# Vision tower with a mixture-of-experts layer on one core: last tiles reordered on ScalarE and GpSimd, weight casts moved behind the search, bias rows moved behind the gates, zero fill moved from step 18 to step 6

## The chip, the cores and the metric

The kernel runs on 1 core of one Trainium2 chip. The metric is the device time of one launch in microseconds. Three runs of the kernel before took 414.73, 414.69 and 413.27 us, a median of 414.69 us.

## What is computed

64 images are cut into 36 patches each, normalized, projected to 256 features, normalized again, and given a class row and position rows. That makes 37 rows per image, 2368 in all. Then come one attention layer and one layer of eight experts:

```python
h = tok(x)                                        # 64 x 37 rows of 256
xa = layernorm(h)
attn = where(eye, -max, (q / 256) @ k.T)          # per image, its own row is masked
h = h + softmax(attn) @ v
x2 = layernorm(h)
probs = softmax(x2 @ router_w + router_b); topv, topi = top_k(probs, 2)
# each expert takes at most 444 (row, slot) pairs, those with the highest gates
hid = gelu(xin @ w1 + b1); out_e = (hid @ w2 + b2) * gate
out = layernorm(scatter_add(out_e)) * ln_g + ln_b
return h + out
```

## The kernel before, in words

**Tiles and steps.** Three images make a tile of 111 rows, so there are 22 tiles (`TILES`). A software pipeline of 28 steps (`SKEW` is 6) works on up to seven tiles at once; every engine has its own `step(i, slot)`, written out by hand, and `pipeline` unrolls the first and last steps and loops over the middle ones. The engines meet at semaphores only, and each engine does its instructions in the written order. In step i, tile i is projected and tile i - 1 is normalized for attention (L636). Tile i - 2 has its scores and its exponential (L666), tile i - 3 its attention output (L1246), and tile i - 4 its second normalization: logits L654, row L595. Its residual row then gets the last bias `ln_b` on GpSimd (L1624, called bias row here).

**SyncE's queue.** One queue in one order carries the loads of x and nearly all stores of the first part. Step i loads tile i + 4 (L442, three pieces of 36 rows) into the buffer that tile i has left (four buffers). It then stores the second normalization of tile i - 4 (L487) and the residual rows of tile i - 6 twice (L506 into `x2_rows`, L509 into `out`). One step also has the zero fill: the two zero blocks (L496), one row of `sums` (L498), and rows 112 to 127 of all 46 blocks of `x2_rows` (L499, from 16 partitions of `zero`). VectorE takes the statistics of tile i + 3 in step i (L1080), in the middle of its step:

```python
                t = i + 3
                if live(t):
                    stats_x(t, (slot + 3) % 4)
```

**Routing.** From step 21 on VectorE also picks each row's two best experts (`best`, L1132 to L1145) and makes the gates (`gates`, L1150 to L1162). This is done for the first 16 tiles within the steps and for the last six behind them. A search in eight rounds then finds each expert's threshold. In a round VectorE counts one part of the keys (L1290) and ScalarE the other (`signs_of`, L707 and L710). The lists of rows follow, and GpSimd gathers the rows (L1649).

**Experts.** Every float32 weight and activation is split in a high part (a cast on ScalarE, `w1_high` L684 and `w2_high` L690) and a low part (a subtraction on VectorE). TensorE multiplies three products of them (L977, L994). SyncE loads the weights behind the stores of the last tiles.

Of the kernel before, what the change touches and what calls it, by code (L numbers as in the profile page):

```python
# [29 lines left out]
ALU = mybir.AluOpType  # L30
# [3 lines left out]
EPS = 1e-5  # L34
# [10 lines left out]
def vit_tower(nc, x, ln1_g, ln1_b, w_proj, b_proj, ln2_g, ln2_b, cls_token, pos_emb,  # L45
# [28 lines left out]
    with ctx:  # L74
# [275 lines left out]
        def live(t):  # L350
            return not isinstance(t, int) or 0 <= t < TILES
# [82 lines left out]
        def _(sp):  # L434
# [42 lines left out]
            def step(i, slot):  # L477
# [10 lines left out]
                if isinstance(i, int) and i == 1:  # L488
# [2 lines left out]
                    load(c_l, b1t[:, :], b1)  # L491
                    sp.dma_start(b2t[:, :], b2.rearrange("a (k p) -> p (a k)", p=128),
                                 allow_slow_non_contiguous=True).then_inc(c_l, 16)
                if isinstance(i, int) and i == 18:
                    sp.wait_ge(s_xz, 5)
                    sp.dma_start(x2_blocks[0:P, 0:2, :], rep(zero[:, :].rearrange("p (a f) -> p a f", a=1), 1, 2))\  # L496
                        .then_inc(s_fill, 16)
                    sp.dma_start(sums[0:1, :], zero[0:1, 0:ED]).then_inc(s_fill, 16)  # L498
                    sp.dma_start(x2_blocks[P:128, :, :],  # L499
                                 rep(zero[0:128 - P, 0:XW].rearrange("p (a f) -> p a f", a=1), 1, Q + 2)).then_inc(s_fill, 16)  # L500
# [62 lines left out]
        def _(act):  # L563
# [34 lines left out]
            def step(i, slot):  # L598
# [31 lines left out]
                t = i + 2  # L630
                if live(t):
                    norm_x(t, (slot + 2) % 4)
                t = i - 1
                if live(t):
                    plain(act, (x1T_ps, t - 1), (h_nb, t + 1))
                    nc.scalar.activation(x1[:, odd, :], tile_of(H, t), ACT.Identity, bias=norm(par, 2, 1),  # L636
                                         scale=norm(par, 1, 1)).then_inc(x1_ok, 1)
                t = i
                if live(t):
                    plain(act, (z_2, t + 1), (n_rs, i + 1))  # L640
                    nc.scalar.activation(tile_of(H, t), z2[:, :], ACT.Copy, scale=norm(par, 1, 0)).then_inc(z_sc, 1)  # L641
                if isinstance(i, int) and i == 1:
                    act.wait_ge(c_qk, 1)
                    nc.scalar.copy(wqk[:, :, :], bank(3)[:, 0:EC * ED].rearrange("p (c e) -> p c e", c=EC)).then_inc(c_tv, 1)
                    nc.scalar.copy(tb[:, :], bank(4)[:, 0:EC]).then_inc(c_tv, 1)
                    nc.scalar.copy(wv[:, :, HW], bank(4)[:, EC:2 * EC]).then_inc(c_tv, 1)
                    nc.scalar.copy(bvb[:, HW:HW + 1], bank(4)[0:P, 2 * EC:2 * EC + 1]).then_inc(c_tv, 1)
                    nc.scalar.copy(wv[:, :, ED:HW], bank(4)[:, 3 * EC:3 * EC + EC * E].rearrange("p (c e) -> p c e", c=EC))\
                        .then_inc(c_tv, 1)
                    nc.scalar.copy(bvb[:, ED:HW], bank(4)[0:P, 3 * EC + EC * E:3 * EC + EC * E + E]).then_inc(c_tv, 1)  # L650
# [7 lines left out]
                    norm_row(i - 5, (slot + 3) % 4, odd)  # L658
                if live(t) and not (isinstance(i, int) and i == TILES + 2):
                    norm_row(t, slot, par)  # L660
                t = i - 2
                if live(t):
                    need(act, s_nmx, t + 1)
                    need(act, pT_ps, t)
                    need(act, g_h, t - 1)
                    nc.scalar.activation(prob[:, :], masked[:, :], ACT.Exp, bias=nmax[:, 0:1], scale=1.0 / ED,  # L666
                                         accum_out=psumr[:, par:par + 1]).then_inc(p_ok, 1)
                t = i - 2
                if live(t):
                    plain(act, (h_dev, t + 1), (v_sb, t + 1))  # L670
                    nc.scalar.activation(tile_of(H, t, ED, HW), v[:, par, HW + 1:VW], ACT.Copy, scale=dev[:, odd:odd + 1])\
                        .then_inc(h_rw, 1)
                t = i - 1
                if live(t):
                    need(act, x1T_ps, t + 1)
                    need(act, s_ps, t - 1)
                    nc.scalar.copy(x1T[:, odd, :], bank(6)[:, 0:EC * P]).then_inc(x1T_sb, 1)  # L677
            pipeline(act, step, 6, 18)

            def w1_high(e, pr):  # L680
# [32 lines left out]
            act.wait_ge(r_odd, 1)  # L713
            for r in range(NR - 1):
                signs_of(r)
                if r >= 3:
                    (w2_high if r % 2 == 0 else w1_high)(0, (r - 3) // 2)

            act.wait_ge(c_pool, 4)
            nc.scalar.copy(hitab[:, :, :], rep(iorow[:, 0:COLS].rearrange("p (c a) -> p c a", a=1), 2, 2)).then_inc(r_tab, 1)  # L720
            nc.scalar.copy(lotab[:, :, :], rep(locen[:, :].rearrange("p (c a) -> p c a", a=1), 2, 2)).then_inc(r_tab, 1)

            act.wait_ge(c_l, N_L)

# [789 lines left out]
        def _(pool):  # L1514
# [77 lines left out]
            def step(i, slot):  # L1592
                par = slot % 2
                on = [k for k, back in enumerate((0, 1, 4)) if live(i - back)]
                if on:
                    last = isinstance(i, int) and i == TILES + 3
                    a, b = (1, 2) if last else (on[0], on[-1] + 1)
# [14 lines left out]
                    for k, done in ((1, h_nb), (2, g_nb)):  # L1612
                        if k == 1 and k in on:
                            G.tensor_tensor(dev[:, par:par + 1], norm(par, 0, 1), norm(par, 1, 1), ALU.mult).then_inc(h_dev, 1)
                        if k in on:
                            k = 1 if last else k
                            G.tensor_scalar(norm(par, 2, k), nmv[:, k, 0:1], norm(par, 1, k), -1.0, ALU.mult, ALU.mult)\  # L1617
                                .then_inc(done, 1)
                for t in range(i - 6, i - 4) if isinstance(i, int) and i == TILES + 3 else (i - 5,):
                    if live(t) and not (isinstance(i, int) and i == TILES + 2):  # L1620
                        if isinstance(t, int) and t == 0:
                            pool.wait_ge(c_l, N_L)
                        need(pool, x2_ok, t + 1)
                        G.tensor_tensor(tile_of(H, t), tile_of(H, t), lnb[:, :], ALU.add).then_inc(hb, 1)  # L1624
# [108 lines left out]
```

## Time and profile before

| what | value |
| --- | --- |
| median of 3 runs | 414.69 us |
| the profiled execution, its own time | 415.01 us |
| its span, first to last instruction | 413.1 us |
| TensorE, VectorE, ScalarE, GpSimd busy | 84%, 76%, 62%, 54% of the span |
| mean granted TensorE clock | 0.913 of 2.4 GHz |
| chain that ended last: TensorE, VectorE, issue, GpSimd | 60%, 14%, 10%, 8% |

The tiles take the span up to about 180 us, routing from there to 235 us, and the experts the rest. Busy shares are means over these three stages. The chain of waits tells which engine set the end of each stage. Times in rows are microseconds from the start of the span.

### The profile page before, as it was taken

The page shows a single profiled execution, that of the slowest core. Times are in us where ns is not written, and L with a number is a line of the kernel's source. Part 1 is how long each engine was busy: PE and PEld are TensorE (multiplying, and loading weights), DVE is VectorE, ACT ScalarE, POOL GpSimd, SP SyncE. Part 2 cuts the span into 40 slices and gives each one's busy share as a digit, 9 for nine tenths or more (in the row PEclk, how much of TensorE's full clock was granted, in tenths as well). Part 3 has the DMA queues.
Part 4 walks back from the last instruction along what each step waited for, and adds up shares of the span by engine and source line. Part 5 has one row for each costly group of instructions (what it writes and reads, how often), then busy time and mean ns, then how long its engine had stood idle before and what let it go on. Part 6 is the DMA issues. An engine that isn't in the chain of part 4 may idle for free.

```text
span 413.1 us, 7904 instructions
## 1 busy us (share of the span) xinstructions
PE 348.5 (84%) x2128; PEld 307.3 (74%) x2128; DVE 315.5 (76%) x874; ACT 255.3 (62%) x552; POOL 224.1 (54%) x377
## 2 busy tenths in 40 slices
PE   2799999999999998731019899999999999999960
PEld 0499988878878886431009899999999999999950
DVE  6763788787878877679879755778888888787954
ACT  3263778767777785454710478677777776868620
POOL 3243676756667665340005443158686877755675
PEclk9896999999999999865555999999999999999995
DMA  6650114454444479768702496546758585852231
GB/s 185 173 115 12 35 55 110 136 154 129 138 141 129 122 123 108 186 198 268 20 0 68 119 274 190 161 151 179 216 173 236 166 235 169 250 169 64 60 84 45
DMA packets 49278, 57.29 MB, mean 139 GB/s; under 512 B 12248, under 2 KB 38229, under 8 KB 49244
## 3 DMA queue, kind: packets, MB, share of 16 engines
q1 hardware_dynamic: 42602, 43.11, 39.4%
q0 software_dynamic: 5568, 13.00, 11.8%
q10 hardware_dynamic: 1074, 0.79, 0.8%
q8 instruction: 14, 0.23, 0.2%
q14 instruction: 20, 0.16, 0.1%
HBM read 36.74 MB, written 21.36 MB: 141 GB/s over the span
## 4 chain that ended last, share of the span: by engine, by line
PE 60%; DVE 14%; issue 10%; POOL 8%; ACT 4%; DMA 1%; ACTq 1%; DVEq 1%; POOLq 0%
PE pall L994 18%; PE pz L977 17%; PE pall L837 6%; DVE wproj L1290 2%; PE pall L805 2%; POOL held L1630 2%; PE pall L812 2%; PE pall L939 2%; PE pall L1005 1%; ACT stage L576 1%; PE pz L785 1%; POOL nrm L1609 1%; PE pall L963 1%; DMA bproj<-in_b_proj 1%; PE pall L777 1%
## 5 line engine op out<-in xcount | busy, mean ns | idle before, releaser
L994 PE MATMUL pall<-halves 128*128 128x444 f32 x384 | 88.6, 365 | 1.9 <-DVE halves L1398 1.9
L977 PE MATMUL pz<-halves 128*128 128x444 f32 x384 | 87.1, 362 | 0.1
L994 PEld LDWEIGHTS pall<-halves 128*128 128x128 f32 x384 | 70.8, 188 | 7.0 <-issue 1.5
L977 PEld LDWEIGHTS pz<-halves 128*128 128x128 f32 x384 | 71.9, 188 | 5.1 <-DVE halves L1409 0.2
L1649 POOL DMA_INDIRECT held<-x_rows,gidx x32 | 36.9, 1152 | 58.8 <-DVE gidx L1339 38.2
L738 ACT ACTIVATE wproj<-pz,b1t 128x444 f32<-128x444 f32 x64 | 40.5, 633 | 44.0 <-PE pz L977 43.4
L1398 DVE TENSOR_TENSOR halves<-wproj,halves 128x444 fp32r<-128x444 f32 x64 | 39.7, 621 | 27.1 <-ACT halves L750 18.7
L837 PE MATMUL pall<-halves 128*112 128x256 f32 x396 | 56.1, 298 | 3.1 <-DVE halves L1089 3.1
L837 PEld LDWEIGHTS pall<-halves 128*112 128x112 f32 x396 | 51.2, 186 | 7.2 <-DVE halves L1089 3.5
L1673 POOL DMA_INDIRECT out<-rows,didx x28 | 37.0, 1323 | 22.1 <-DVE rows L1446 15.5
L750 ACT CAST halves<-wproj 128x444 fp32r<-128x444 f32 x64 | 36.1, 564 | 2.0
L1657 POOL DMA_INDIRECT rows<-sums,sidx x28 | 30.3, 1080 | 7.8 <-issue 7.5
L1368 DVE TENSOR_TENSOR halves<-stage,halves 128x512 fp32r<-128x512 f32 x32 | 22.0, 688 | 7.1 <-ACT halves L684 7.1
L636 ACT ACTIVATE x<-held,nrm 112x256 f32 (+1 forms) x22 | 13.2, 601 | 22.1 <-POOL nrm L1617 12.7
L576 ACT ACTIVATE stage<-stage,rs 112x768 f32<-112x768 f32 x22 | 22.6, 1027 | 6.9 <-POOL rs L1554 6.9
L805 PE MATMUL pall<-x1T,wq 128*128 128x112 f32 x176 | 25.0, 285 | 0.8 <-ACT x1T L677 0.3
L812 PE MATMUL pall<-wv,x1T 128*112 128x273 f32 x88 | 24.9, 406 | 0.0
L1607 POOL TENSOR_SCALAR nrm<-nmv 112x3 f32<-112x3 f32 (+2 forms) x26 | 6.2, 238 | 33.5 <-DVE nmv L1187 27.6
L1254 DVE BATCH_NORM_STATS2 hstat<-held 112x6 f32 (+1 forms) x22 | 9.4, 428 | 19.6 <-POOL held L1630 19.5
L805 PEld LDWEIGHTS pall<-x1T,wq 128*128 128x128 f32 x176 | 21.4, 191 | 3.3 <-ACT x1T L677 2.4
L1630 POOL TENSOR_TENSOR held<-held,posb 112x256 f32 (+1 forms) x22 | 16.0, 728 | 14.4 <-ACT held L641 14.4
L1080 DVE BATCH_NORM_STATS2 xstat<-stage 112x6 f32<-112x384 f32 x44 | 22.3, 548 | 1.7 <-DMA stage<-in_x 1.7
(283 smaller groups left out, 744.5 us busy)
## 6 DMA issues: line engine op xcount, KB each, us to landing
stage<-in_w SPq DMA_DIRECT2D x32, 512.0 KB
stage<-in_x SPq DMA_DIRECT2D x64, 108.0 KB
x_rows<-x SPq DMA_DIRECT2D x22, 224.0 KB, 2.9
x_rows<-held SPq DMA_DIRECT2D x22, 224.0 KB, 4.1
sums<-rows SPq DMA_DIRECT2D x7, 448.0 KB
out<-held SPq DMA_DIRECT2D x21, 111.0 KB
x_rows<-zero SPq DMA_DIRECT2D x1, 1474.9 KB
wproj<-in_w_proj ACTq DMA_DIRECT2D x1, 768.0 KB
```

What stands on the lines that cost most here:

```text
L576: nc.scalar.activation(xn, xin[:, slot, :], ACT.Identity, bias=rs[:, 0, 2:3], scale=rs[:, 0, 1:2]).then_inc(x_n, 1)
L738: nc.scalar.activation(hr[:, k % 2, 0:CAP], bank(k % 2)[:, 0:CAP], ACT.Gelu, bias=col(b1t, u)).then_inc(u_sb, 1)
L750: nc.scalar.copy(hh[:, k % 2, 0:CAP], hr[:, k % 2, 0:CAP]).then_inc(h_hi, 1)
L805: m = nc.tensor.matmul(bank(3)[:, o * P:(o + 1) * P], wqk[:, c, o * 128:(o + 1) * 128], xt_[:, c, :], start=(c == 0), stop=(c == EC - 1))
L812: m = nc.tensor.matmul(bank(4)[0:P, 0:VW], xt_[:, c, :], wv[:, c, :], start=(c == 0), stop=(c == EC - 1))
L837: nc.tensor.matmul(bank(2)[0:P, 0:ED], xs[:, c * P:(c + 1) * P], w[:, c, :], start=(c == k == 0), stop=False)
L977: m = nc.tensor.matmul(bank(k % 2)[:, 0:CAP], w[:, c, k * 128:(k + 1) * 128], xs[:, e % 2, c, 0:CAP], start=(n == 0), stop=(n == 3 * EC - 1))
L994: m = nc.tensor.matmul(pall[:, 2 * (e % 2) + o, 0:CAP], w[:, k, o * 128:(o + 1) * 128], hs[:, k % 2, 0:CAP], start=(k == 0 and n == 0), st ...
L1398: V_.tensor_tensor(hl[:, k % 2, 0:CAP], hr[:, k % 2, 0:CAP], hh[:, k % 2, 0:CAP].bitcast(fp32), ALU.subtract)\
L1649: pool.indirect_dma_start(xg[:, e % XB_N, j, :], None, x2_rows, bass.IndirectOffsetOnAxis(ap=gidx[:, k:k + 1], axis=0)).then_inc(g_in[e % ...
L1657: pool.indirect_dma_start(prev[:, j, :], None, sums[0:1 + e * SLOTS, :], bass.IndirectOffsetOnAxis(ap=sidx[:, k:k + 1], axis=0)).then_inc( ...
L1673: pool.indirect_dma_start(out, bass.IndirectOffsetOnAxis(ap=didx[0:n, k:k + 1], axis=0), final_of(e)[0:n, j, :], None, bounds_check=IMAGES ...
```

## The change

It moves four things and adds no arithmetic. The zero fill is issued in step 6 of SyncE instead of step 18. ScalarE does `residual_row(20)` behind the scaling of tile 21 in step 21, and in step 22 the exponential of tile 20 and the copy `turned(21)` before the logits and the row of tile 18. GpSimd makes the two normalizations of step 22 one after the other, each behind its own wait, and does the bias rows of tiles 18 and 19 in step 23 and those of 20 and 21 behind the last gates. The first expert's four casts come behind the search.

```diff
-                if isinstance(i, int) and i == 18:
+                if isinstance(i, int) and i == 6:
                     sp.wait_ge(s_xz, 5)
                     sp.dma_start(x2_blocks[0:P, 0:2, :], rep(zero[:, :].rearrange("p (a f) -> p a f", a=1), 1, 2))\
...
-                t = i - 1
-                if live(t):
+                def residual_row(t):
                     plain(act, (x1T_ps, t - 1), (h_nb, t + 1))
...
+                last = isinstance(i, int) and i == TILES
+                if live(i - 1) and not (isinstance(i, int) and i == TILES - 1):
+                    residual_row(i - 1)
+                if last:
+                    exponentials(i - 2)
+                    turned(i - 1)
                 t = i
                 if live(t):
                     plain(act, (z_2, t + 1), (n_rs, i + 1))
                     nc.scalar.activation(tile_of(H, t), z2[:, :], ACT.Copy, scale=norm(par, 1, 0)).then_inc(z_sc, 1)
+                if isinstance(i, int) and i == TILES - 1:
+                    residual_row(i - 1)
...
+                if live(i - 2) and not last:
+                    exponentials(i - 2)
...
+                if live(i - 1) and not last:
+                    turned(i - 1)
...
             for r in range(NR - 1):
                 signs_of(r)
-                if r >= 3:
-                    (w2_high if r % 2 == 0 else w1_high)(0, (r - 3) // 2)
...
+            for pr in range(2):
+                w1_high(0, pr)
+                w2_high(0, pr)
...
                 on = [k for k, back in enumerate((0, 1, 4)) if live(i - back)]
+                if isinstance(i, int) and i == TILES:
+                    on = [2]
+                    pool.wait_ge(x1_ok, i - 2)
+                    pool.wait_ge(h_rw, i - 2)
+                    pool.wait_ge(h_mv, i)
+                    link(G.tensor_scalar(nrm[:, par, 0, 1:2], nmv[:, 1:2, 1], EPS, None, ALU.add))
+                    link(G.tensor_tensor(nrm[:, par, 1, 1:2], nrm[:, par, 0, 1:2], neghalf[:, :], ALU.pow))
+                    G.tensor_scalar(norm(par, 2, 1), nmv[:, 1, 0:1], norm(par, 1, 1), -1.0, ALU.mult, ALU.mult).then_inc(h_nb, 1)
+                    G.tensor_tensor(dev[:, par:par + 1], norm(par, 0, 1), norm(par, 1, 1), ALU.mult).then_inc(h_dev, 1)
...
-                for t in range(i - 6, i - 4) if isinstance(i, int) and i == TILES + 3 else (i - 5,):
-                    if live(t) and not (isinstance(i, int) and i == TILES + 2):
+                if isinstance(i, int) and i == TILES + 4:
+                    pool.wait_ge(r_V, 2)
+                for t in {TILES + 1: (i - 5, i - 4), TILES + 2: (), TILES + 3: (), TILES + 4: (i - 6, i - 5)}.get(i, (i - 5,)) \
+                        if isinstance(i, int) else (i - 5,):
+                    if live(t):
```

**SyncE, around step 6**, as the built programs have it. The load after the fill is that of tile 11, in step 7:

```order
@@ -32,4 +32,7 @@
 L442 DMA stage<-in_x 36x768 x3
 L487 DMA x_rows<-x 112x2x256
+L496 DMA x_rows<-zero 112x2x513
+L498 DMA sums<-zero 1x256
+L499 DMA x_rows<-zero 16x46x513
 L506 DMA x_rows<-held 112x2x256
 L509 DMA out<-held 111x256
```

The three transfers of the fill moved in front of the first stores of residual rows and of all loads of x from tile 11 on.

**ScalarE in step 22, before**, from the residual row of tile 21 (L636) to the copy that ends its step (L677):

```order
L636 ACTIVATE x<-held,nrm 112x256
L654 ACTIVATE LG<-held,nrm 112x8
L595 ACTIVATE x<-held,nrm 112x256
L666 ACTIVATE prob,psumr<-masked,nmax 112x112
L671 ACTIVATE held<-v,dev 112x8
L677 COPY x1T<-pall 128x224
```

and the same step in the changed program, where L635, L647, L641 and L674 are the lines of the residual row, the exponential, the copy and the logits:

```order
L635 ACTIVATE x<-held,nrm 112x256
L647 ACTIVATE prob,psumr<-masked,nmax 112x112
L641 COPY x1T<-pall 128x224
L674 ACTIVATE LG<-held,nrm 112x8
L595 ACTIVATE x<-held,nrm 112x256
L686 ACTIVATE held<-v,dev 112x8
```

The exponential and the copy moved ahead of two operations of tile 18.

## Rows read from the trace of the kernel before

**Rows 1.** The page: shares of the span in the chain that ended last, by engine.

```profile
PE 60%; DVE 14%; issue 10%; POOL 8%; ACT 4%; DMA 1%; ACTq 1%; DVEq 1%; POOLq 0%
```

**Rows 2.** Windows: stretch, length, busy PE, PEld, DVE, ACT, POOL, clock, DMA share, GB/s.

```profile
150.00:152.00 2.00, 2.00 (x18) 1.88 (x16) 0.71 (x4) 1.85 (x5) 1.72 (x4) 1.00 0.90 101
...
164.00:166.00 2.00, 1.89 (x13) 1.52 (x12) 1.83 (x8) 0.99 (x4) 0.00 (x0) 1.00 0.89 206
```

**Rows 3.** Timeline of SyncE's queue from the fill on: start, us, transfer.

```profile
147.49 0.74 SPq L499 DMA_DIRECT2D x_rows<-zero  x1
148.27 0.79 SPq L506 DMA_DIRECT2D x_rows<-held  x1
...
153.02 3.85 SPq L487 DMA_DIRECT2D x_rows<-x  x1
```

**Rows 4.** Transfers of `x_rows`: landing times of those issued at 148.27 and at 153.02.

```profile
DMA to landing us min/median/max: 18.6/18.6/18.6
...
DMA to landing us min/median/max: 17.7/17.7/17.7
```

**Rows 5.** DMA issues on the page: KB of each, and median landing time where known.

```profile
stage<-in_x SPq DMA_DIRECT2D x64, 108.0 KB
x_rows<-x SPq DMA_DIRECT2D x22, 224.0 KB, 2.9
...
out<-held SPq DMA_DIRECT2D x21, 111.0 KB
x_rows<-zero SPq DMA_DIRECT2D x1, 1474.9 KB
```

**Rows 6.** Timeline of SyncE's queue around step 6.

```profile
69.20 0.46 SPq L506 DMA_DIRECT2D x_rows<-held  x1
...
70.09 1.22 SPq L442 DMA_DIRECT2D stage<-in_x  x3
```

**Rows 7.** Timeline of VectorE and ScalarE in step 8.

```profile
78.92 1.01 DVE L1080 BATCH_NORM_STATS2 xstat<-stage 112x6 f32<-112x384 f32 x2
...
80.25 0.14 DVE L1241 SCALAR_TENSOR_TENSOR nmax<-v,nm 112x1 f32<-112x1 f32 x1
...
81.15 0.37 ACT L666 ACTIVATE prob<-masked,nmax 112x112 f32<-112x112 f32 x1
```

**Rows 8.** Windows, columns as in rows 2: where the clock changes its level.

```profile
170.50:171.00 0.50, 0.50 (x6) 0.50 (x6) 0.26 (x2) 0.00 (x0) 0.01 (x1) 0.84 0.53 158
...
217.50:218.00 0.50, 0.46 (x6) 0.49 (x6) 0.50 (x2) 0.00 (x0) 0.00 (x0) 0.50 0.00 0
225.00:225.50 0.50, 0.50 (x5) 0.50 (x4) 0.50 (x1) 0.00 (x0) 0.29 (x1) 0.55 0.42 160
```

**Rows 9.** Timeline of step 22.

```profile
166.11 0.23 POOL L1607 TENSOR_SCALAR nrm<-nmv 112x2 f32<-112x2 f32 x1 [2.62 <-DVE nmv L1187]
...
167.78 0.16 DVE L1241 SCALAR_TENSOR_TENSOR nmax<-v,nm 112x1 f32<-112x1 f32 x1
...
169.05 0.37 ACT L666 ACTIVATE prob<-masked,nmax 112x112 f32<-112x112 f32 x1
```

**Rows 10.** Timeline from 180 us: `best` beside the bias rows and behind them.

```profile
180.26 0.74 DVE L1132 TENSOR_TENSOR LG<-LG,rbb 112x48 f32<-112x48 f32 x1 [1.52 <-ACT LG L654]
...
181.31 0.38 DVE L1135 TENSOR_TENSOR eqm<-LG,m 112x48 f32<-112x48 f32 x1
181.72 0.65 DVE L1136 TENSOR_TENSOR eqm<-eqm,erev 112x48 f32<-112x48 f32 x1
...
183.43 0.21 DVE L1135 TENSOR_TENSOR eqm<-lg,m 112x48 f32<-112x48 f32 x1
...
187.43 0.62 DVE L1276 TENSOR_SCALAR keysa<-scratch 128x896 int32<-128x896 int32 x1
```

**Rows 11.** Timeline of ScalarE: a cast within the search, and its next work behind the search.

```profile
197.71 0.60 ACT L684 CAST halves<-stage 128x512 fp32r<-128x512 f32 x1
...
228.40 0.53 ACT L732 CAST halves<-pall 128x448 fp32r<-128x448 f32 x1 [20.20 <-PE pall L953]
```

More of the change, by code:

```diff
@@ L637, in step, with turned, exponentials @@
                                          scale=norm(par, 1, 1)).then_inc(x1_ok, 1)
+                def turned(t):
+                    need(act, x1T_ps, t + 1)
+                    need(act, s_ps, t - 1)
+                    nc.scalar.copy(x1T[:, odd, :], bank(6)[:, 0:EC * P]).then_inc(x1T_sb, 1)
+                def exponentials(t):
+                    need(act, s_nmx, t + 1)
+                    need(act, pT_ps, t)
+                    need(act, g_h, t - 1)
+                    nc.scalar.activation(prob[:, :], masked[:, :], ACT.Exp, bias=nmax[:, 0:1], scale=1.0 / ED,
+                                         accum_out=psumr[:, par:par + 1]).then_inc(p_ok, 1)
+                last = isinstance(i, int) and i == TILES
[4 more added lines that the diff above has]
+                    turned(i - 1)
                 t = i
@@ L660, in step @@
                     norm_row(t, slot, par)
[L661 to L667, printed above, removed]
+                if live(i - 2) and not last:
+                    exponentials(i - 2)
                 t = i - 2
@@ L672, in step @@
                         .then_inc(h_rw, 1)
[L673 to L677, printed above, removed]
+                if live(i - 1) and not last:
+                    turned(i - 1)
             pipeline(act, step, 6, 18)
```

## The prediction, written before the changed kernel ran

> **What bounds the kernel now.** I read the chain of waits first. TensorE holds 60% of it [rows 1], and through the tiles and the experts the chain hardly leaves it. A stop in another engine that TensorE has to wait for is therefore not won back later. Then I read the timeline of SyncE's queue, because one of the four moves puts a large transfer ahead of loads that VectorE needs, and last the timeline of steps 21 to 27 and of the search. There ScalarE, VectorE and GpSimd hand work to each other and TensorE waits.
>
> **The zero fill.** In the kernel before it is issued in step 18, when all of x has been loaded. Its large part is 1474.9 KB [rows 5], issued at 147.49 [rows 3]. From 150 to 164 us the transfers move about 100 GB/s at a share of 0.90, and then 206 GB/s [rows 2]: 1510 kB at 98 to 101 GB/s is 15.2 us, so in that stretch the fill moves alone, and it has drained at about 164.2, 16.7 us after its issue. What is issued behind it does not land before that: the store issued at 148.27 took 18.6 us and the one issued at 153.02 took 17.7 us [rows 3, 4], where the median of such a store is 2.9 us [rows 5]. Even issuing a transfer takes 3.85 us then [rows 3]. In step 18 nobody waits for these stores.
>
> In step 6 somebody does. The fill comes where the store of residual rows is now issued, at 69.20, and its large part 0.89 us later, at 70.1. Behind it stand the two stores of tile 0 (335 KB) and then the three pieces of tile 11's load, 324 KB, which are issued at 70.09 now [rows 5, 6]. VectorE takes the statistics of tile 11 at 78.92, in the middle of step 8, without having waited [rows 7]. When does the load land? The two ends are these:
> - Early: the fill drains at 70.1 + 16.7 = 86.8, and a landing of 2.5 us, a little under the median of the stores, gives 89.3.
> - Late: the store issued at 153.02 ended 559 KB behind the fill and landed at 170.7, 23.2 us after the fill's issue. The load ends 659 KB behind it, 100 KB more, at 206 GB/s 0.5 us: 70.1 + 23.7 = 93.8.
> - Between: 86.8, then 659 KB at 206 GB/s (3.3 us), then 2 us for the landing: 92.1.
>
> I take 92.5, near the late end, since that is a landing and the others are put together. VectorE then stands for 92.5 - 78.9 = 13.6 us. Behind L1080 it has the maximum of tile 6's scores (L1241), on which ScalarE's exponential waits. That one ended at 80.39 and the exponential began at 81.15 [rows 7], so 0.8 us of the stop is hidden. **12.8 us lost.** TensorE can finish its projection and turns, which need nothing from behind L1080, and then stands too.
>
> Such a stop should also cost the clock its upper level. In the drain of the pipeline, with pauses between its matmuls, TensorE fell from 2.4 to 1.2 GHz at 170.8; after the search it was busy from 217.5 and came back at 225.4 only, 7.9 us of work at the lower level [rows 8]. TensorE sets the pace in these steps, so half of what it works at the lower level is lost: nothing if the clock stays up, 4 us if it takes as long to come back. I take **3.0 us**, nearer to the second, since the stop is much longer than the pauses before 170.8.
>
> The load of tile 12 is issued right behind the backlog, at about 92, and should land at 99 to 100. VectorE needs it about 6.5 us after it goes on, at 99 or later with the slow clock: at most 1 us more, which I keep for the range.
>
> A page speaks to the drain. The Trainium skill, SBUF — State Buffer, section "Door 1: The DMA port swizzle", says that a transfer's rate follows from how many of 16 ports its partitions reach, at 27.2 GB/s each. The fill reads 16 neighbouring partitions, four ports, which is an estimate of 109 GB/s and 13.9 us; the trace has 98 to 101 GB/s. By it the stop would be 1.4 us shorter and the sum so much less, and it gives no reason why the fill should run faster in step 6.
>
> **Steps 21 and 22.** In step 22 GpSimd starts its two normalizations at 166.11, when the later one (tile 18, L1187) is there [rows 9]. Now tile 21's no longer waits for that one, so its residual row comes earlier and is out of ScalarE's way when the maximum comes. The exponential of tile 20 began at 169.05, though its maximum was there at 167.94 [rows 9]: 1.1 us, in which ScalarE did tile 18's two operations. They are behind it now. The copy that opens TensorE's step 24 follows it. From step 21 comes 0.2 us more, as the position rows of tile 21 start earlier on GpSimd and get out of the way of `best`. That is 1.3 us. If TensorE's clock still falls at 170.8 [rows 8], up to 0.8 us more, since the matmuls of tile 21 then stand ahead of the fall; but ScalarE's operations of tile 19 end this gain. **I take 1.5 us gained**, with ends at 0.8 and 2.1.
>
> **Bias rows.** Three of them run on GpSimd beside the `best` of the last six tiles. There L1135 takes 0.38 us, and 0.21 us at 183.43 with nothing beside it; L1132 takes 0.74 us for the same 48 elements [rows 10], where by L1135's 0.21 it should take about 0.22. That is 0.7 us. L1136 between them has the same kind of operands and fills the time from 181.7 to 182.4, 0.65 us instead of 0.21: in all **1.1 us gained**, since these operations stand in the chain. Two bias rows now start when the last gates are made, beside L1276 at 187.43 [rows 10], which the search waits for. The trace has no bias row beside an operation of this kind. The cost lies between nothing and one bias row of 0.7 us. I take 0.2, nearer to nothing, because L1276 follows on its own engine at once, and GpSimd has to see a semaphore first. The Trainium skill, GPSIMD Engine Reference, section "Key points", says that the two engines contend where VectorE has two inputs in SBUF or runs in a two-port mode. The slow L1132 and L1135 agree with this, and L1276, with one input and 0.62 us for 896 elements, would be of the second sort; by this rule alone the whole 0.7 us could be due and the sum 0.5 us more.
>
> The two last residual stores, and behind them the weight loads and the gate stores, go out 3 us later on SyncE. The gathers come at 220 us, some 10 us after the gate stores would land, and this cover is ample.
>
> **Casts.** Each takes 0.60 us, and came when ScalarE's part of a round was done and VectorE's count and TensorE's sum were still to come. So they cost nothing within the search. Behind it four of them take 2.4 us of the 20.20 us in which ScalarE is idle until 228.40 [rows 11]. Nothing either way.
>
> **Sum.** 12.8 + 3.0 - 1.5 - 1.1 + 0.2 = +13.4 us. On the profiled execution's own 415.0 us this gives 428.4; the median of the runs is 0.3 us below it, so **428.0 us**.
>
> **Rivals.**
> - *The load is in time* (0.08). Transfers behind the fill would be served beside it. It decides at the landing of tile 11's load: up to 79.7 nothing is lost. Only the gains are left, 2.4 us: 412.3 us, faster. For it: the x loads are read from another memory than the fill. Against it: 18.6 and 17.7 us, on the same queue [rows 4].
> - *The fill drains faster in step 6* (0.06), at the 206 GB/s seen behind it [rows 2]: 7.3 us instead of 15.2 us, so everything behind it comes 7.9 us earlier, the load at about 84.6; a loss of 4.9 us, no fall of the clock: 417.2 us, just slower.
> - *Two stops* (0.12): the load of tile 12 is also late, or the clock stays down for the full 8 us. 1 to 3 us more than forecast: 429 to 431 us.
> - *No clock loss* (0.10): TensorE does not fall, or has slack in these steps: 425 us.
>
> The forecast itself has 0.64. What cannot be told from no change is 0.5% or 2 us. Faster by more than that is most of the first rival, 0.07; no change the rest of it and a part of the second, 0.04; slower 0.89. With the clock lost, the ends of the stall case are 10.4 - 0.8 + 1.7 - 2.1 - 1.1 = +8.1 (1.7 us is a return after 3.4 us) and 14.9 - 0.8 + 4 - 0.8 - 0.4 + 1 = +17.9, that is 422.8 and 432.6 us. To hold 8 in 10 the range goes a little below: 421 to 432.5.
>
> **What would show it.** In the changed profile VectorE's L1080 should wait over 10 us on the load of x, once, near 80 us, with TensorE idle and at 0.5 behind it, and transfers at 100 GB/s from 72 to 87. `best` at the end should run without its 0.74 us operation, the exponential of step 22 should follow its maximum at once, and the rounds of the search should stay as long as they are. If L1080 never waits, the prediction is wrong in its main term.

## The result, and the profile after

The changed kernel takes 426.47 us (median of six runs, 423.87 to 428.82), the kernel before 414.06 us in the runs beside it (413.21 to 415.46). The ratio is 1.0295 with a 95% interval of 1.0247 to 1.0343: **slower by 3%**, where 428.0 us (421 to 432.5) and slower were forecast. The profiled execution of the changed kernel took 428.82 us with a span of 426.9 us and a mean granted clock of 0.896. It is the slowest of the six. Executions of one kernel differ by up to 6 us in the runs of this document. Between its traces 4 us arise ahead of the statistics of tile 9 alone (62.8 to 66.6 us). So the kernels are compared below by stretches between two events of the same trace, and whole times by their medians.

The timeline of SyncE's queue from step 6 on, in the changed kernel, answers to [rows 3, 6]. Columns are the start, the length and the transfer:

```profile
69.71 0.69 SPq L499 DMA_DIRECT2D x_rows<-zero  x1
70.45 0.79 SPq L506 DMA_DIRECT2D x_rows<-held  x1
71.28 3.83 SPq L509 DMA_DIRECT2D out<-held  x1
75.16 13.15 SPq L442 DMA_DIRECT2D stage<-in_x  x3
88.37 0.48 SPq L487 DMA_DIRECT2D x_rows<-x  x1
```

The windows, with the columns of [rows 2]:

```profile
76.00:78.00 2.00, 2.00 (x16) 1.68 (x15) 1.91 (x6) 1.78 (x5) 0.99 (x3) 1.00 0.90 98
...
82.00:84.00 2.00, 0.00 (x0) 0.00 (x0) 0.00 (x0) 0.00 (x0) 0.00 (x0) 1.00 0.90 98
84.00:86.00 2.00, 0.00 (x0) 0.00 (x0) 0.00 (x0) 0.00 (x0) 0.00 (x0) 0.79 1.08 96
...
88.00:90.00 2.00, 0.00 (x0) 0.00 (x0) 0.00 (x0) 0.00 (x0) 0.00 (x0) 0.50 0.79 239
95.00:100.00 5.00, 4.36 (x15) 3.53 (x16) 3.39 (x12) 3.26 (x10) 2.82 (x8) 0.50 0.50 163
100.00:105.00 5.00, 5.00 (x33) 4.46 (x33) 3.59 (x14) 2.57 (x8) 2.52 (x6) 0.78 0.40 108
```

And the timeline of the other engines as they go on. What stands in brackets is the idle time before the operation and what ended it:

```profile
93.63 1.02 DVE L1093 BATCH_NORM_STATS2 xstat<-stage 112x6 f32<-112x384 f32 x2 [14.98 <-DMA stage<-in_x]
...
95.11 0.39 ACT L647 ACTIVATE prob<-masked,nmax 112x112 f32<-112x112 f32 x1 [14.22 <-DVE nmax L1254]
...
95.64 0.44 PE L913 MATMUL pall<-ident,prob 112*112 112x112 f32 x1 [13.82 <-ACT prob L647]
```

L1093 is the line that was L1080 before. The fill drains at 98 GB/s and a share of 0.90 in step 6 too, with nothing moving beside it. Two stores and a load stick behind it: issuing the three pieces of tile 11 alone takes 13.15 us. VectorE waits 14.98 us for that load, from 78.65 on, and 3.2 us after its stop the last engine, TensorE, stands too. TensorE's clock falls from 2.4 to 1.2 GHz at 85 us, and is back at 102.

At the end of the tiles the timeline shows step 22, to be held against [rows 9], and the start of `best`, to be held against [rows 10]. L1254, L647 and L1145 were L1241, L666 and L1132:

```profile
182.50 0.16 DVE L1254 SCALAR_TENSOR_TENSOR nmax<-v,nm 112x1 f32<-112x1 f32 x1
...
182.69 0.39 ACT L647 ACTIVATE prob<-masked,nmax 112x112 f32<-112x112 f32 x1 [0.32 <-DVE nmax L1254]
...
192.78 0.21 DVE L1145 TENSOR_TENSOR LG<-LG,rbb 112x48 f32<-112x48 f32 x1 [1.50 <-ACT LG L674]
```

The exponential follows its maximum 0.03 us after that has ended, where it came 1.11 us late, and the first operation of `best` takes 0.21 us instead of 0.74.

The chain of waits shows something new in the search. Its pieces are given in order of time, as start, length and what held the chain:

```profile
206.82 5.89 SPq L450
...
213.76 19.14 DMA x_rows<-gate
...
234.09 1.23 POOL held L1674
```

VectorE's operation that makes the first list of indices began at 231.41 and ended at 231.56, but GpSimd's first gather (L1674) could not begin: it needs the gates in `x_rows`, and the last of the four gate stores, issued at 213.76, landed at 232.9 only. Counted from the start of that operation, the gather comes 2.68 us after the list, where it came 0.47 us after it before. Then its row named the list as what it had waited for:

```profile
220.50 1.82 POOL L1649 DMA_INDIRECT held<-x_rows,gidx  x1 [38.19 <-DVE gidx L1339]
```

**Where the 13.8 us went.** The two profiled spans (413.1 and 426.9 us), cut at events that both traces have. Tile 9 is the last whose statistics come ahead of the fill; the searches run from their first count to the first list:

| stretch | before | after | difference |
| --- | --- | --- | --- |
| to the statistics of tile 9 | 66.6 | 66.3 | -0.4 |
| to those of the last tile | 77.1 | 92.5 | +15.4 |
| to the last logits' bias | 36.5 | 34.0 | -2.5 |
| to the first count of the search | 8.4 | 7.2 | -1.1 |
| to the first list | 31.4 | 31.4 | 0.0 |
| to the first gather | 0.5 | 2.7 | +2.2 |
| to the first matmul of an expert | 10.7 | 9.9 | -0.8 |
| to the end | 181.9 | 182.9 | +1.0 |

The last line is the clock again. It was up from 235.4, TensorE then waited for gathered rows (the longest time 0.92 us, up to 241.81), and at 242.2, as the experts begin, it fell again until 249.0:

```profile
240.00:245.00 5.00, 4.08 (x42) 3.80 (x41) 3.20 (x10) 0.62 (x2) 0.34 (x1) 0.72 0.17 46
245.00:250.00 5.00, 5.00 (x17) 4.22 (x16) 2.99 (x7) 2.87 (x6) 4.08 (x4) 0.60 0.63 195
```

The other traces bear this out. In the eight in which the clock is up when the experts begin, and stays up, the last stretch takes 181.9 us, and in the six in which it falls again there it takes 182.4 to 182.9.

### The profile page after: what moved, and what is told of

The parts are those of the page before. It is cut to its first block, busy times and chain, and to the rows that moved or that the text cites. A ratio compares the mean times of both kernels' runs of the same rounds, so it can differ in the third digit from the quotient of the medians.

```text
span 426.9 us, 7906 instructions
## 1 busy us (share of the span) xinstructions
PE 351.4 (82%) x2128; PEld 310.8 (73%) x2128; DVE 315.3 (74%) x874; ACT 256.3 (60%) x552; POOL 224.4 (53%) x379
## 4 chain that ended last, share of the span: by engine, by line
PE 58%; issue 9%; DVE 8%; POOL 8%; DMA 8%; SPq 4%; ACT 3%; DVEq 0%; POOLq 0%; ACTq 0%
PE pz L990 18%; PE pall L1007 17%; PE pall L850 7%; DMA x_rows<-gate 4%; PE pall L818 3%; DMA stage<-in_x 2%; PE pall L825 2%; SPq L450 2%; POOL held L1655 2%; PE pall L1018 1%; PE pz L798 1%; SPq L442 1%; PE pall L976 1%; PE pall L790 1%; POOL nrm L1631 1%
## 5 line engine op out<-in xcount | busy, mean ns | idle before, releaser
L990 PE MATMUL pz<-halves 128*128 128x444 f32 x384 | 89.2, 369 | 0.0
L990 PEld LDWEIGHTS pz<-halves 128*128 128x128 f32 x384 | 73.6, 192 | 5.1
L1674 POOL DMA_INDIRECT held<-x_rows,gidx x32 | 35.4, 1107 | 55.7 <-issue 41.9
L850 PE MATMUL pall<-halves 128*112 128x256 f32 x396 | 57.2, 302 | 2.6 <-DVE halves L1102 2.6
L850 PEld LDWEIGHTS pall<-halves 128*112 128x112 f32 x396 | 52.2, 187 | 5.7 <-DVE zbias L1121 2.4
L1698 POOL DMA_INDIRECT out<-rows,didx x28 | 37.0, 1323 | 22.1 <-DVE rows L1459 15.5
L1093 DVE BATCH_NORM_STATS2 xstat<-stage 112x6 f32<-112x384 f32 x44 | 22.3, 548 | 17.3 <-DMA stage<-in_x 17.3
L1381 DVE TENSOR_TENSOR halves<-stage,halves 128x512 fp32r<-128x512 f32 x32 | 22.0, 686 | 7.1 <-ACT halves L696 6.1
L635 ACT ACTIVATE x<-held,nrm 112x256 f32 (+1 forms) x22 | 13.2, 601 | 17.1 <-POOL nrm L1639 8.6
L1655 POOL TENSOR_TENSOR held<-held,posb 112x256 f32 (+1 forms) x22 | 16.1, 733 | 13.1 <-ACT held L659 13.1
L1631 POOL TENSOR_TENSOR nrm<-nrm,neghalf 112x3 f32<-112x3 f32 (+2 forms) x26 | 20.9, 804 | 2.3 <-POOL nrm L1629 0.2
L1387 DVE TENSOR_TENSOR halves<-stage,halves 128x512 fp32r<-128x512 f32 x32 | 22.0, 688 | 0.0
```

What stands on the lines that cost most here:

```text
L850: nc.tensor.matmul(bank(2)[0:P, 0:ED], xs[:, c * P:(c + 1) * P], w[:, c, :], start=(c == k == 0), stop=False)
L990: m = nc.tensor.matmul(bank(k % 2)[:, 0:CAP], w[:, c, k * 128:(k + 1) * 128], xs[:, e % 2, c, 0:CAP], start=(n == 0), stop=(n == 3 * EC - 1))
L1631: G.tensor_tensor(nrm[:, par, 1, a:b], nrm[:, par, 0, a:b], rep(neghalf[:, :], 1, b - a), ALU.pow)\
L1674: pool.indirect_dma_start(xg[:, e % XB_N, j, :], None, x2_rows, bass.IndirectOffsetOnAxis(ap=gidx[:, k:k + 1], axis=0)).then_inc(g_in[e % ...
L1698: pool.indirect_dma_start(out, bass.IndirectOffsetOnAxis(ap=didx[0:n, k:k + 1], axis=0), final_of(e)[0:n, j, :], None, bounds_check=IMAGES ...
```

## The experiments

Edits are against the changed kernel, unless it says that they are against the kernel before. Each ratio is against runs of the kernel before on the same chip.

**1. Is it the fill, and it alone?** The fill goes back to step 18 in the changed kernel, and alone to step 6 in the kernel before.

```diff
-                if isinstance(i, int) and i == 6:
+                if isinstance(i, int) and i == 18:
```

> The changed kernel with the zero fill back in step 18 of SyncE's queue and nothing else undone. My theory: the stop of VectorE in step 8 (15.0 us in the changed profile) goes with it, the tail keeps its 3.6 us, and up to 2.2 us of these are given back where the gathers wait for the late gate stores. That gives 410.5 to 413 us, a ratio to before of 0.992 to 0.998. The rival, that the other three moves cost time too, expects 416 us or more.

> The kernel before with the zero fill in step 6 and nothing else. My theory: the whole loss is the fill's, 15 us or a little more without the tail's gain: 428 to 430 us, ratio 1.034 to 1.039, with VectorE waiting 14 to 15 us once on the load of tile 11. The rival, that the loss comes from the fill and another part together, expects clearly less, 420 us or so.

With the fill back: 413.43 us, ratio 0.9974 (0.9929 to 1.0020). With the fill alone: 426.67 us, ratio 1.0308 (1.0236 to 1.0379), a little faster than the 428 to 430 us expected. The stop is in the one and not in the other; with the fill alone VectorE's row reads

```profile
91.11 1.02 DVE L1080 BATCH_NORM_STATS2 xstat<-stage 112x6 f32<-112x384 f32 x2 [15.30 <-DMA stage<-in_x]
```

So the fill's place makes nearly all of the loss. But the other three moves should have won 2.4 us, and the first kernel does not show it: no difference can be told. Its stretches give the reason. It has the short end of the tiles (34.0 and 7.2 us), and then its first gather begins 5.9 us after its list, at 220.17, and 1.2 us after its last gate store has landed (218.97). In the changed kernel too the gather came 1.2 us after that landing. At most 2.2 us were expected to be given back here.

**2. Is it the order of one queue, or the engines that all queues share?** ScalarE's queue issues the large part, at the end of its step 5; the two small transfers stay with SyncE.

```diff
+                if isinstance(i, int) and i == 5:
+                    act.wait_ge(s_xz, 5)
+                    nc.scalar.dma_start(x2_blocks[P:128, :, :], ...
```

> The changed kernel with the large piece of the fill (1475 KB) issued from ScalarE's queue at the end of its step 5 instead of from SyncE's, so that loads of x run on another queue of the same 16 engines. Theory of order (the load waits because it stands behind the fill in one queue): the load of tile 11 is in time or under 3 us late, 411 to 415 us. Rival theory of throughput (the fill fills the engines or the memory's ports, whichever queue it is on): VectorE still stops 8 us or more, 420 us or more.

418.35 us, ratio 1.0115 (1.0043 to 1.0187). That is between the two forecasts. The stop is shorter but not gone, and the tile before is hit:

```profile
59.16 0.39 ACTq L690 DMA_DIRECT2D x_rows<-zero  x1
...
59.64 8.35 SPq L442 DMA_DIRECT2D stage<-in_x  x3
...
78.03 1.02 DVE L1096 BATCH_NORM_STATS2 xstat<-stage 112x6 f32<-112x384 f32 x2 [8.77 <-DMA stage<-in_x]
```

Both are true. With a queue of its own the fill no longer holds up all that follows for 15 us. But the load beside it, issued at once, still takes 8.35 us to issue. From 60 to 75 us the transfers together move 117 to 120 GB/s at a share of 0.92 to 0.96. The Trainium skill, DMA: Bandwidth & Descriptors, section "Queues, rings and completion order", says that each engine takes turns between the queues it has work for, packet by packet. The trace agrees in kind: served in turn, the load is late by 8.8 us, neither by nothing nor by 15.

**3. Small portions.** The large part goes out as six transfers, 8 of its 46 blocks each (6 in the last), in SyncE's steps 3 to 8; the two small transfers stay in step 6.

```diff
+                if isinstance(i, int) and 3 <= i < 9:
+                    sp.wait_ge(s_xz, 5)
+                    qa = 8 * (i - 3)
+                    qb = min(qa + 8, Q + 2)
+                    sp.dma_start(x2_blocks[P:128, qa:qb, :], ...
```

> The changed kernel with the large piece of the fill cut in six (8 of 46 blocks each, about 257 KB, 2.6 us at 98 GB/s), one in each of steps 3 to 8. Same queue, same bytes, same rate. Theory of order and length: each piece delays the loads behind it by less than their lead of about 9 us, no stop: 410.5 to 413 us. Rival: if it is the amount moved in the first steps that counts, the loads of tiles 7 to 12 come late one after the other and 5 us or more are lost, 416 us or more.

412.97 us, ratio 0.9992 (0.9950 to 1.0034). VectorE waits 3.4 us in all for loads of x between 60 and 100 us, and the stretch from tile 9 to the last takes 79.3 us, 2.1 more than before. The same bytes, in steps 3 to 8, cost 2.1 us instead of 15.4. A stop of 2.52 us is left at tile 11, where a part and the two small transfers (the larger of them 449 KB) stand in one step. The kernel of experiment 5 that has them in step 18 takes 77.3 us for this stretch, 0.2 more than before.

**4. Is the drain bound by the 16 partitions it reads?** The fill stays whole in step 6 and on SyncE, but 32 of its 46 blocks are read from 32 partitions and 14 from 14.

```diff
-                    sp.dma_start(x2_blocks[P:128, :, :],
-                                 rep(zero[0:128 - P, 0:XW].rearrange("p (a f) -> p a f", a=1), 1, Q + 2)).then_inc(s_fill, 16)
+                    for qa, qb, p0 in ((0, 32, 0), (32, Q + 2, 64)):
+                        sp.dma_start(x2_blocks[P:128, qa:qb, :].rearrange("p q f -> q p f"),
+                                     rep(zero[p0:p0 + qb - qa, 0:XW].rearrange("p (a f) -> p a f", a=1), 1, 128 - P))\
+                            .then_inc(s_fill, 16)
```

> The changed kernel, fill still in step 6, with the same bytes written from other partitions: rows 112 to 127 of 32 blocks from 32 partitions of the zeros (0 to 31) and those of the other 14 blocks from 14 partitions (64 to 77), instead of all 46 blocks from 16 partitions. Theory: the fill runs at 98 GB/s because 16 neighbouring partitions feed it. With 32 it should run at about twice that, so that VectorE's stop falls from 15 to 7 to 10 us and the time to 417 to 421 us. Rival: the rate is set by the writes of 2052 bytes into DRAM, whatever the source; then the stop stays 14 to 15 us and the time 425 to 428 us.

420.23 us, ratio 1.0193 (1.0145 to 1.0241): the stop is 10.96 us instead of 14.98, a little more than the 7 to 10 expected.

```profile
70.00:75.00 5.00, 5.00 (x38) 4.11 (x37) 3.92 (x14) 4.29 (x13) 3.14 (x7) 1.00 1.02 134
75.00:80.00 5.00, 3.36 (x27) 2.87 (x26) 0.18 (x2) 1.68 (x4) 2.10 (x5) 1.00 0.84 135
```

134 GB/s instead of 98, so the source does set a part of the rate. But this mean hides two parts, as shorter windows show:

```profile
70.00:72.00 2.00, 2.00 (x18) 1.69 (x16) 1.19 (x5) 1.90 (x8) 1.47 (x4) 1.00 0.96 187
72.00:74.00 2.00, 2.00 (x15) 1.66 (x14) 1.73 (x8) 1.66 (x5) 0.79 (x3) 1.00 1.09 90
74.00:76.00 2.00, 2.00 (x17) 1.76 (x17) 1.18 (x4) 1.00 (x2) 1.71 (x5) 1.00 0.92 159
```

The piece that is read from 32 partitions is issued first, at 66.24, and up to 72 us the transfers move 187 GB/s or more, nearly twice the 98. Behind that it is 90 to 159. By the rule of the Trainium skill that the prediction cites (SBUF — State Buffer, "Door 1: The DMA port swizzle"), 32 neighbouring partitions reach eight ports, an estimate of 218 GB/s. The trace comes near it up to 72 us, with 187 GB/s, and not in the mean. The windows do not tell which piece moves when; the edit also splits the fill in two, reads the second piece from 14 partitions and changes the order in which it writes. So what holds the rest is left open.

**5. Why do the three good moves win nothing?** The gate stores are issued early by SyncE: the first 16 tiles' at the head of its step 24, the last six's at the head of step 26, ahead of the last rows and of the weight loads. In the first kernel the fill is in step 18, in the second in six parts in steps 3 to 8 with its small transfers in step 18, in the third still in step 6.

```diff
+                if isinstance(i, int) and i in (TILES + 2, TILES + 4):
+                    n = (i - TILES) // 2
+                    sp.wait_ge(r_V, n)
+                    store_gates(*((0, EARLY), (EARLY, TILES))[n - 1])
...
-            for a, b, n in ((0, EARLY, 1), (EARLY, TILES, 2)):
-                sp.wait_ge(r_V, n)
-                store_gates(a, b)
```

> The changed kernel with the fill back in step 18, and the gate stores taken ahead on SyncE's queue: those of the first 16 tiles at the head of its step 24, those of the last six at the head of step 26, before the last residual stores and the weight loads. My theory: in the run with only the fill back the first gather came 5.9 us after its index list, because the gate stores landed late. Here it should follow its list by about 0.5 us as before, and the tail's 3.6 us come through: 409.5 to 411.5 us, ratio 0.989 to 0.995. The rival (the gathers wait for the bias rows' stores or the weight loads, or the casts now wait for their weights) expects a gap of 3 us or more and no gain.

> The changed kernel with the large piece of the fill in six parts in steps 3 to 8, its two small transfers in step 18, and the gate stores taken ahead. The first spread version had tile 11's statistics 2.6 us late, where the 460 KB block and a part stood in one step; with that block elsewhere no stop is left. Theory: front part as before, tail 3.6 us shorter, gather 0.5 us behind its list: 409.5 to 411.5 us, ratio 0.989 to 0.995. Rival: spreading leaves small delays of the loads in several steps, 1 to 3 us in all.

> The changed kernel, fill still in step 6, with only the gate stores taken ahead on SyncE's queue. Theory: the first gather follows its list by 0.5 us instead of 2.7, and the stop of 15 us stays: 423 to 425 us, about 2 us under the changed kernel. Rival: the gather waits for the last residual stores as long as for the gates, and nothing is gained.

The first: 409.50 us, ratio 0.9896 (0.9850 to 0.9942). The second: 409.17 us, 0.9891 (0.9849 to 0.9933). The third: 423.78 us, 1.0261 (1.0209 to 1.0313). Its interval overlaps that of the changed kernel (1.0247 to 1.0343), so the gain shows in the stretches and not in the whole time. From the list to the gather it is now 1.7, 0.5 and 0.5 us. The gather in the second, and TensorE in the third in the windows in which the changed kernel was partly at the lower level:

```profile
214.54 1.83 POOL L1679 DMA_INDIRECT held<-x_rows,gidx  x1 [31.16 <-DVE gidx L1357]
```

```profile
240.00:245.00 5.00, 4.50 (x42) 3.81 (x40) 3.94 (x15) 1.53 (x3) 1.32 (x2) 1.00 0.02 5
245.00:250.00 5.00, 3.88 (x20) 3.56 (x20) 2.93 (x5) 3.38 (x7) 4.39 (x3) 1.00 0.90 282
```

In the second and third the gather waits for its list again, the clock stays up as the experts begin, and the stretch behind takes 181.9 us as before. The gate stores had been the hidden bound: in each of the six traces in which the last of them lands after the list (the changed kernel, those with the fill back, on ScalarE's queue or in portions, and the two of experiment 6), the gather begins 1.2 us after that landing. In the first kernel of this experiment they land at 209.6, 3.4 us ahead of the list, and another store takes their place. The last `out` rows are issued behind them and land at 213.62, and the gather begins 1.0 us later:

```profile
207.15 6.47 DMA out<-held
```

**6. Each good move alone**, against the kernel before: the bias rows only, and the reordering of steps 21 and 22 on ScalarE and GpSimd only. Both edits are those of the diff at the top.

> The kernel before with the move of the bias rows alone (18 and 19 in step 23, 20 and 21 behind the last gates). Theory: the last picks run without GpSimd beside them, 1.1 us less from the last logits to the first count of the search, 7.2 to 7.3 us instead of 8.4; the two bias rows cost the search nothing, since they have to wait for VectorE's L1276; but the last residual stores and the gate stores behind them go out later, and the first gather comes 1 to 3 us after its list instead of 0.5. In all 412.5 to 416 us, nothing that can be told from no change. Rival: the bias rows beside the search cost 0.7 us.

> The kernel before with the new order of steps 21 and 22 on ScalarE and GpSimd alone. Theory: from the statistics of tile 21 to the last logits 34.0 us instead of 36.5, as in the changed profile; the gate stores do not come earlier by as much, since SyncE's queue is behind then, and the gather gives back up to 1 us: 411 to 413.5 us. Rival: the 2.5 us came from the missing fill in the tail, and stay away here.

The bias rows: 414.81 us, ratio 1.0020 (0.9988 to 1.0052). They win their 1.1 us in the end of `best`, and the gather then waits 2.1 us instead of 0.5. The reordering: 414.07 us, ratio 0.9990 (0.9954 to 1.0025), above the 411 to 413.5 us expected. It wins 2.1 us (34.5 instead of 36.5), loses 1.4 in the search (32.8 instead of 31.4) and 2.9 in front of the gather. In the search it is this row of ScalarE:

```profile
194.68 0.62 ACT L696 CAST halves<-stage 128x512 fp32r<-128x512 f32 x1 [2.56 <-DMA stage<-in_w]
```

The cast stands between two rounds, and here the weights that it converts had not landed. In the kernel before the first cast, at 197.71 [rows 11], did not wait.

**7. What the move of the casts is worth.** The second kernel of 5 again, and beside it the same with the four casts back in the rounds.

```diff
                 signs_of(r)
+                if r >= 3:
+                    (w2_high if r % 2 == 0 else w1_high)(0, (r - 3) // 2)
...
-            for pr in range(2):
-                w1_high(0, pr)
-                w2_high(0, pr)
```

> The same kernel as the one with the fill in six parts and early gate stores, beside the next one. Both theories: 408 to 410.5 us, 0.7 to 1.4% below the kernel before; search 31.4 us from its first count to the first list.

> That kernel with the four casts back in the rounds of the search. My theory: moving the casts gains nothing by itself, but it is what lets the weight loads come late on SyncE's queue. There the first weight load is issued at 202.22 us, behind the early gate stores and the last rows, and such a load takes 7.8 us to land, while round 3 of ScalarE ends at 191.9 and round 4 begins at 193.2. So the first cast, now behind round 3, waits until about 210 and the search is longer by 15 to 18 us: 46.5 to 49.5 us instead of 31.4, and the whole 423 to 428 us. Rival, that the casts are only 0.6 us each of work and hidden in the rounds, as the prediction counted them: search 31.4 us, whole 408 to 411 us.

The first: 409.82 us, ratio 0.9916 (0.9888 to 0.9944). With the casts back: 425.46 us, 1.0284 (1.0233 to 1.0336). The search takes 47.7 us instead of 31.4:

```profile
193.86 0.19 ACT L727 ACTIVATION_READ_ACCUMULATOR junka<-keysa,canda 128x1 f32 x1
211.54 0.62 ACT L701 CAST halves<-stage 128x512 fp32r<-128x512 f32 x1 [17.50 <-DMA stage<-in_w]
```

The weight loads go out at 203.90 there, behind the early gate stores. A cast in the round makes the search wait for them. Behind the search it waits for nothing.

The version with the fill in six parts, early gate stores and late casts beats both kernels in two sets of runs: 1.1% and 0.8% below the kernel before, with both intervals below 1, and some 4% below the changed one.

## Why the prediction was right, and where it was wrong

**The stop, right in mechanism, 1.2 us too short.** The fill drained at the forecast rate, the load of tile 11 landed at 93.6 where 92.5 was taken and 93.8 was the late end, and TensorE stood. From the fill's issue to the landing it took 23.9 us, a little over the 23.7 of the late end. The estimate near the late end, from a landing seen in the trace, was the better one; the sum put together from pieces was short. VectorE's wait was 14.98 us where 13.6 was taken. Counted from tile 9's statistics in each trace, the exponential behind it came 14.3 us late and TensorE's first matmul behind it 14.0 us. So 0.8 us was hidden at ScalarE, as forecast, and 1.1 us at TensorE, and 14.0 stands against the term of 12.8.

**The clock, right in the event and at first in the price, but not all of it stayed lost.** It fell at 85 us and was back at 102, after 6.6 us of matmuls from 95.6 on, near the upper end of what was taken. These rows are the turn of the exponentials' output in two successive steps, first in the kernel before (L900), then in the changed one (L913):

```profile
82.02 0.26 PE L900 MATMUL pall<-ident,prob 112*112 112x112 f32 x1
...
88.48 0.26 PE L900 MATMUL pall<-ident,prob 112*112 112x112 f32 x1
```

```profile
95.64 0.44 PE L913 MATMUL pall<-ident,prob 112*112 112x112 f32 x1 [13.82 <-ACT prob L647]
...
105.08 0.26 PE L913 MATMUL pall<-ident,prob 112*112 112x112 f32 x1
```

Against tile 9's statistics (66.62 and 66.26) TensorE is 14.0 us late at the first row and 17.0 at the second: the lower level cost the 3.0 us of the term, and "half of what it works at the lower level is lost" came out as 3.0 of 6.6. In the same operation of the next four steps TensorE is 16.1, 15.8, 15.6 and 15.5 us late, and at the last tile 15.4. So it won 1.6 us back, and 1.4 of the 3.0 was left. With the fill alone it is 14.3, 16.9 and at the end 15.4. The step that failed is the one at the head of the prediction, that a stop in another engine that TensorE has to wait for "is therefore not won back later". What makes the steps behind the stop shorter than before was not tried. The two terms stand for 15.8 us in the sum and came to 15.4, since the stop was 1.2 us longer than its term and the clock 1.6 us cheaper.

**Two stops, ruled out.** Tile 12's load was in time. **The load in time** and **the faster drain** fell with the 98 GB/s. **No clock loss** has a half truth in it: there was a fall, and less than half of its price stayed.

**Steps 21 and 22: 2.5 us instead of 1.5.** The new order without the other moves gives 2.1 (experiment 6), the end that was given, and the clock has a hand in both numbers. In the kernel before it fell at 170.8 [rows 8], 27.1 us behind the statistics of the last tile, was back at 174.2 and fell again at 177.7. In the changed kernel those statistics come at 158.74, and the clock stays up until 191.0, 32.3 us behind them. With the fill alone the order is the old one, and the clock is up there too. The windows at that place, in the kernel before, with the fill alone, and in the changed kernel:

```profile
171.00:174.00 3.00, 3.00 (x11) 2.38 (x11) 0.55 (x2) 1.50 (x5) 1.74 (x4) 0.50 0.68 185
```

```profile
181.00:184.00 3.00, 2.25 (x15) 1.65 (x13) 2.77 (x11) 2.00 (x9) 0.00 (x0) 1.00 0.40 113
184.00:187.00 3.00, 1.42 (x9) 0.80 (x7) 2.67 (x12) 1.60 (x7) 1.77 (x4) 1.00 0.28 83
```

```profile
185.00:190.00 5.00, 2.39 (x12) 1.15 (x10) 4.69 (x21) 2.68 (x9) 2.48 (x5) 1.00 0.58 168
```

With the fill alone the stretch takes 35.3 us and not 36.5, and in the changed kernel 34.0. So with the clock up at this place the order is worth 1.3 us, the working of the prediction, and 1.2 of the 2.5 us come without it. From the first matmul of L805 there to the last of L829 it is 4.6 us in the kernel before (from 169.99) and 2.9 with the fill alone (from 182.24), so it is the clock that shows. The fill is not in step 18 there either, and no run parts the two.

**Bias rows: 1.1 us, exact.** The 0.2 us for a collision in front of the search was not due:

```profile
198.81 1.90 POOL L1649 TENSOR_TENSOR held<-held,lnb 112x256 f32<-112x256 f32 x2 [6.03 <-DVE V L1175]
...
198.82 0.62 DVE L1289 TENSOR_SCALAR keysa<-scratch 128x896 int32<-128x896 int32 x1
```

L1289 was L1276 and takes the 0.62 us of before [rows 10]. GpSimd pays: of its two rows, the one beside L1289 takes 1.2 us and the other the 0.7 that one takes alone. So what the prediction cites of the Trainium skill (GPSIMD Engine Reference, "Key points") does not show on VectorE's side here.

**The gates: the step that was wrong.** "This cover is ample" it said of the gate stores, landed "some 10 us" ahead of the gathers. The prediction had no row of a gate store's landing and put none together. Before, the last is issued at 199.8 and lands after 15.6 us, at 215.4, 4.6 us ahead of the list. In the changed kernel it is issued 13.9 us later (at 213.76), while the list comes 11.4 us later, and takes 19.1 us: 2.5 and 3.5 us used up the 4.6 and 1.4 more. With the 1.2 us from the landing to the gather, the gather lost 2.2 us, the clock behind it about 1. That is the term missing in the sum, and experiments 5 and 6 show that it also hides what the good moves win. That the total came so near is in part luck, since errors stand against each other: +1.2 (the stop) and +2.2 (the gates), with the +1.0 of the clock behind them, against -1.6 (the clock at the stop), -1.0 (steps 21 and 22) and -0.2 (the collision). The -0.8 between gather and first matmul and the -0.4 of the start have no cause that was tried. Together this is +0.4: 13.8 us between the spans, where 13.4 was the sum. Two small slips of the prediction change nothing: its own terms give 428.1 us and not 428.0, and by its figures for the ports the stop is 1.3 us shorter and not 1.4.

**The casts: right here, and incomplete.** "Nothing either way" holds in the changed kernel, whose search takes the 31.4 us of before; no run has the changed kernel with the casts left in the rounds. But a cast in the search also waits for a load. In the kernel before the first cast begins 10.1 us after its load's issue at 187.57; with the reordering alone it waited until 194.68, 7.3 us after an issue at 187.41. So the cover was some 3 us, an estimate from these two, and the prediction did not name it. Where the weights come later it costs 1.4 us or 16 us (experiments 6 and 7).

## What to carry to other kernels

A large transfer without a reader nearby is not free: ask what is queued behind it and by when that is needed, and cut it into portions that fit between two loads. For each gain on a path, write down the landing time of everything that the next stage also waits for, small stores of single numbers above all; a path shortened by 3.6 us gained nothing until the stores beside it were issued earlier too. Moving such a store ahead of others can put another in its place, so look again at what comes last. And a loss is not all there at the end: follow one operation through the steps behind a stop, to see what is won back. Work that depends on a load should not stand inside a loop on the critical path, even if it is short and hidden.

## What was not expected of the hardware

- A gate store carries 2.6 or 7.0 KB and takes 12.4 to 19.1 us to land in the two kernels, where the median of a row store of 224 KB is 2.9 us [rows 5]. Why it takes so long no run tried. In the changed kernel the landing comes long after the transfers have gone quiet, as the window with its share of 0.00 shows:

```profile
222.00:226.00 4.00, 1.38 (x4) 0.71 (x4) 2.66 (x6) 0.00 (x0) 0.00 (x0) 0.50 0.14 0
226.00:230.00 4.00, 1.07 (x12) 1.10 (x13) 3.73 (x13) 0.00 (x0) 0.00 (x0) 0.50 0.00 0
```

- Issuing such a store takes up to 5.89 us of SyncE's queue, and the four together 12.2 us (204.68 to 216.91). Where they go out early (experiments 5 and 7), the rows and weights behind them are late by such times.
- After the stop TensorE worked 6.6 us at the lower level and was 3.0 us further behind by it; 1.6 of these it had won back at the last tile. Most of the loss was the idle time itself.
